# Attention scores in one orientation instead of two, on one Trainium2 core

## The reference

```python
xn = layernorm(x)
q_latent, kv_latent = xn @ wq_down, xn @ wkv_down            # 192 and 64 wide
q = concat(q_latent @ wq_nope, rope(q_latent @ wq_rope))     # 16 heads, 128 + 64
k = concat(kv_latent @ wk_nope, rope(kv_latent @ wk_rope))
v = kv_latent @ wv_up                                        # 16 heads, 192
probs = softmax(where(causal, q @ k.T / sqrt(192), -inf))    # per batch and head
x + (probs @ v) @ wo + expert_mix(xn)     # 32 gated experts, top 8 of them per token
```

## Time and profile before

| Profiled execution | |
|---|---|
| device time | 1277.71 us |
| span of the trace | 1275.9 us |
| mean granted clock of the matrix engine | 0.985 |
| matrix engine busy | 1216.7 us (95%), 5952 products |
| VectorE busy | 898.6 us (70%) |
| ScalarE busy | 589.5 us (46%) |
| GpSimd busy | 682.0 us (53%) |

### The profile page before, as it was taken

One profiled execution on the slowest core, in us unless ns is written; L12 is line 12 of the kernel. 1 busy time (PEld: TensorE's weight loads), 2 busy tenths in 40 slices (PEclk: granted clock), 3 DMA queues, 4 the chain that ended last, 5 costly groups with the idle time before them and its releaser, 6 DMA issues. The chain is left out here.

```text
span 1275.9 us, 20266 instructions
## 1 busy us (share of the span) xinstructions
PE 1216.7 (95%) x5952; PEld 809.1 (63%) x5952; DVE 898.6 (70%) x1410; ACT 589.5 (46%) x1192; POOL 682.0 (53%) x546
## 2 busy tenths in 40 slices
PE   5899899999999999999999999979999999999997
PEld 3555465555565555555655555547888887888886
DVE  6679879879889888888888798664544444544444
ACT  3454536545546445456355365443434343333332
POOL 1176667677677667767776676552233333233332
PEclk9988999999999999999999999998999999999999
DMA  5001001001000000000000001006533334433332
GB/s 202 34 1 33 1 1 33 1 1 32 0 0 17 15 0 15 16 0 2 30 0 0 15 0 58 1 26 180 163 115 107 110 115 114 127 109 115 115 115 90
DMA packets 26442, 67.33 MB, mean 53 GB/s; under 512 B 3044, under 2 KB 9700, under 8 KB 26408
## 3 DMA queue, kind: packets, MB, share of 16 engines
q1 hardware_dynamic: 26264, 66.84, 17.4%
q10 hardware_dynamic: 144, 0.07, 0.0%
HBM read 62.42 MB, written 4.47 MB: 52 GB/s over the span
## 5 line engine op out<-in xcount | busy, mean ns | idle before, releaser
L734 ACT ACTIVATE ring<-ps_s 128x512 f32<-128x512 f32 (+3 forms) x320 | 146.5, 468 | 302.3 <-PE ps_s L601 301.2
L1333 POOL TENSOR_TENSOR hl<-hf,hh 128x512 fp32r<-128x512 f32 x96 | 123.5, 1286 | 288.2 <-ACT hh L1270 288.2
L897 DVE TENSOR_REDUCE nm<-ps_m 128x1 f32<-128x512 f32 (+3 forms) x370 | 197.8, 550 | 47.0 <-PE ps_m L569 42.1
L1060 POOL TENSOR_TENSOR first<-first,ring 128x512 f32<-128x512 f32 (+3 forms) x160 | 159.5, 997 | 83.8 <-ACT ring L734 51.2
L1029 POOL TENSOR_TENSOR xtf<-xtf,sinv 128x512 f32<-128x512 f32 x62 | 85.3, 1375 | 119.3 <-DVE xtf L851 119.3
L1302 DVE TENSOR_TENSOR gs<-gs,routing 128x512 f32<-128x512 f32 x64 | 44.3, 692 | 137.8 <-ACT gs L1266 137.8
L908 DVE TENSOR_TENSOR first<-first,ring 128x512 f32<-128x512 f32 (+3 forms) x160 | 133.1, 832 | 9.7 <-ACT ring L734 4.9
L613 PE MATMUL ps_o<-ring,kvn 128*64 128x512 f32 (+3 forms) x640 | 132.6, 493 | 0.0
L598 PE MATMUL ps_s<-shift,ones 128*128 128x512 bf16 (+3 forms) x384 | 126.7, 330 | 0.2 <-ACT first L734 0.2
L1270 ACT ACTIVATE hh<-hf 128x512 fp32r<-128x512 f32 x96 | 60.7, 633 | 122.0 <-DVE hf L1307 122.0
L1266 ACT ACTIVATE gs<-ps_g 128x512 f32<-128x512 f32 x96 | 57.4, 598 | 121.4 <-PE ps_g L1225 121.4
(11 more groups left out here) (241 smaller groups left out, 3104.3 us busy)
## 6 DMA issues: line engine op xcount, KB each, us to landing
routing<-wT_scratch SPq DMA_DIRECT2D x34, 256.0 KB, 3.7
raw_a<-in_e SPq DMA_DIRECT2D x17, 384.0 KB, 3.0
cosv<-in_e SPq DMA_DIRECT2D x17, 384.0 KB, 3.0
sinv<-wT_scratch SPq DMA_DIRECT2D x17, 384.0 KB, 3.6
raw<-in_e SPq DMA_DIRECT2D x17, 384.0 KB, 3.0
routing<-wT_scratch SPq DMA_DIRECT2D x16, 384.0 KB, 3.3
raw_a<-in_a SPq DMA_DIRECT2D x8, 512.0 KB, 3.4
raw_b<-in_b SPq DMA_DIRECT2D x8, 480.0 KB, 4.0
```

What stands on the lines that cost most here:

```text
L734: nc.scalar.activation(probs(k, e), ps_s[(2 * k + e) % 3][:, off:], ACT.Exp, scale=SCALE).then_inc(exp_done, 1)
L897: nc.vector.tensor_reduce(out=to, in_=bank[:, 0:keys], axis=AXX, op=ALU.max, negate=True).then_inc(piece_max, 1)
L1060: nc.gpsimd.tensor_tensor(first[:, c, 1, off:], first[:, c, 1, off:], probs(k, 1), ALU.add).then_inc(sum_pool, 1)
L1333: nc.gpsimd.tensor_tensor(hl[:, c, :], hf[:, c, :], hh[:, c, :].bitcast(F32), ALU.subtract).then_inc(h_lo, 1)
```

## The change

The scores are computed once, with **queries on partitions**. The unit is now a tile `t` of 128 queries (8 per stage, `TILES`) with all its `(t + 1) * 128` keys as the moving operand. A tile over more than 512 keys (`t >= 4`) goes as two halves of equal width into two neighbouring banks. So the eight banks are now two per head for scores (`ps_s`), two for transposes (`ps_t`), `ps_o` and one `ps_x`.

- VectorE reduces both halves of a head's scores in one instruction to `nm`, the negated maximum (`maximum`).
- ScalarE takes the exponential with `nm` as bias, and the same instruction gives the row sum into `lsum` (`exponent`). The scale is folded into the keys in `prepare`.
- The probabilities are then turned, 128 by 128, by the matrix engine (`turn`, with `ident`), and copied to SBUF by ScalarE (bank `ps_t0`) or VectorE (bank `ps_t1`) (`take_turned`), and only then multiplied with the values (`values`), now 128 queries at a time.
- VectorE inverts the 8 columns of sums (`invert`), ScalarE spreads them (`widen`), the matrix engine turns them (`spread`), ScalarE copies them (`take_reciprocals`), and VectorE multiplies.
- Gone are the 24 pieces and their maxima, `shift` and its product, `add_probs` on VectorE and GpSimd, the product with ones, and the reciprocal over 512 columns.

The first six projections go to six different free banks (`start_banks`). The core of the diff:

```diff
+            def scores(i, b, t, e, half):
...
+                if half == 0:
+                    ge(pe, exp_done, u - 1)
...
+                nc.tensor.matmul(out[:, 0:width], qhi[b][e][:, q], khi[b][e][:, kk], start=not diagonal, stop=False, skip_group_check=True)
+                nc.tensor.matmul(out[:, 0:width], qhi[b][e][:, q], klo[b][e][:, kk], start=False, stop=False, skip_group_check=True)
+                mm = nc.tensor.matmul(out[:, 0:width], qlo[b][e][:, q], khi[b][e][:, kk], start=False, stop=True, skip_group_check=True)
+            def turn(s, t, e, g):
+                x = g if t >= TPC else e
+                before = s * TURNS_PER_S + turns_before(t) + (e if t >= TPC else 0)
+                pe.wait_ge(exp_done, s * U + 2 * t + e + 1)
+                ge(pe, copied[x], before)
+                for at, j in enumerate(groups_of(t)[g]):
+                    mm = nc.tensor.transpose(ps_t[x][:, at * P:(at + 1) * P], prob[t % 2][e][:, j * P:(j + 1) * P], ident[:, :])
+                mm.then_inc(turned[x], 1)
+            def values(s, b, t):
+                for x in range(2):
+                    pe.wait_ge(copied[x], s * TURNS_PER_S + turns_before(t + 1))
...
+                for j in range(t + 1):
+                    for e in range(2):
+                        mm = nc.tensor.matmul(ps_o[64 * e:64 * e + 64, at], kvn[:, b * 8 + j, :], pt[t % 2][:, e, j, :], start=j == 0, stop=j == t)
...
+                        else:
+                            for e in range(2):
+                                scores(i, b, t, e, 0)
+                                scores(i, b, t, e, 1)
+                            turn(sp, tp, 0, 0)
+                            turn(sp, tp, 0, 1)
+                            also(("KR1", "Yp1", "WA")[t - TPC - 1])
+                            turn(sp, tp, 1, 0)
+                            turn(sp, tp, 1, 1)
+                            if t == TILES - 1:
+                                also("Y0")
+                            values(sp, bp, tp)
+                            also(("QL1", "B", "Y1")[t - TPC - 1])
...
+                nc.scalar.activation(prob[t % 2][e][:, 0:len(halves) * width].rearrange("p (h k) -> p h k", k=width),
+                                     ps_s[e][:, 0:len(halves), 0:width], ACT.Exp, bias=nm[:, e:e + 1],
+                                     accum_out=lsum[:, t // TPC, t % TPC, e:e + 1]).then_inc(exp_done, 1)
...
+                        exponent(s, t, 0)
+                        if t > TPC:
+                            take_turned(sp, tp, 0, 0)
...
+                        if has and (t == 0 or t > TPC):
+                            take_turned(sp, tp, 1, 0)
+                        exponent(s, t, 1)
...
+                        if 0 < t < TPC:
+                            maximum(s, t, 0)
+                            take_turned(sp, tp, 1, 0)
```

More of the change, by code:

```diff
@@ L303, in misc_order @@
             got.append((b, name))
+            if last and b and name == "Lp":
+                got += [(b, turn) for turn in TURNS]
     return got
@@ L603, in values @@
-            def values(s, b, k, alone=False):
-                c, j, off, _ = step_of(k)
-                last = k in (TPC - 1, STEPS - 1)
-                if j == 0:
-                    ge(pe, o_copied, s * 2 + c)
-                for e in range(2):
-                    if e or alone:
-                        pe.wait_ge(exp_done, s * U + 2 * k + e + 1)
-                    nc.tensor.matmul(ps_o[64 * e:64 * e + 64, off:], kvn[:, b * 8 + j, :], probs(k, e),
-                                     start=j == 0, stop=last).then_inc(pv_done, 1)
@@ L627, in row_sums, with spread @@
-            def row_sums(i, b, name, s, c):
-                for e in range(2):
-                    pe.wait_ge(*sums(s, c, 7 if c else 3, e))
-                def products(out):
-                    for e in range(2):
-                        mm = nc.tensor.matmul(out[64 * e:64 * e + 64, :], ones[:, 0:64], first[:, c, e, :], start=True, stop=True)
+                        mm = nc.tensor.transpose(out[0:E, j * P:(j + 1) * P], w2[:, g * TPC + j, :], ident[:, :])
                     return mm
                 side(i, b, name, products)
+            def spread(out):
+                for t in range(TPC):
+                    mm = nc.tensor.transpose(out[:, t * P:(t + 1) * P], rec[:, t * P:(t + 1) * P], ident[:, :])
+                return mm
@@ L640, in project_out @@
                 pe.wait_ge(olo_done, s * 2 + c + 1)
[L642 to L647 removed]
+                side(i, b, name, lambda out: out_products(out, m))
             def body(i):
@@ L694, in _ @@
             for name in PROLOGUE:
                 project(0, None, name, 0, 0)
-            for n in range(NP):
-                piece(0, n, 0)
             pairs_loop(pe, body)
-            s = 2 * PAIRS - 1
-            values(s, 1, STEPS - 1, alone=True)
-            n = BEFORE_LAST + len(LAST)
+            s, t = 2 * PAIRS - 1, TILES - 1
             for e in range(2):
-                pe.wait_ge(*sums(s, 1, 7, e))
+                for g in range(2):
+                    turn(s, t, e, g)
+            pe.wait_ge(widened, s * 2 + 2)
```

732 lines of the change are left out of this document (345 added, 387 removed).

## The result

The changed kernel takes 1356.9 us (median of 4 runs, 1353.41 to 1367.88), the kernel before 1276.46 us. The ratio is 1.0643, with a 95% interval of 1.0579 to 1.0707: slower by 6.4%. Beside two of the later kernels it was timed once more: 1357.7 us, ratio 1.0627 (1.0603 to 1.0651). The forecast was 1333 us, its own range 1300 to 1365. The profiled execution took 1353.4 us at a span of 1351.6.

The account below looks back on a forecast made before the run. The matrix engine bounds the kernel, hardly waiting. Profiled 1277.7 us, +64 for 15 longer stages, -5.7 start, -4 first stage, +1.8 last stage gives 1334, median 1333 us; own range 1300 to 1365, overall 1225 to 1410.

Parts of the forecast that it names:

- the 0.5 us allowed for row sums: Each stage: 0.5 us added for the exponential's row sums and for double waits in front of an instruction.
- the third rival: Value products: up to 32 dense 128-column records run slower than 0.053 us each; 1398 us, at the far end 1460; chance 11%.
- first product: Start: first score product waits only for GpSimd's low part, ready at 69.35 us instead of starting at 75.04: -5.7 us.
- first stage: First attention stage: no turns and values of an earlier stage, so -4 us.
- 14 stages: Attention stages at 53.9 us each: 43.0 of matrix-engine work, 10.4 of waits, 0.5 for the rest.
- last stage, to the output product: Last stage without projections: 36.7 us to the last score, then tile 7's chain, together 44.8 against 43.0 before: +1.8 us.
- The second rival: Tiles 0 to 3: waits drop the clock, 6 us of work per stage at 1.2 GHz; +48 us, 1381 us; chance 14%.
- the 4 us that I took off: First stage: 4 us less because it has no turns and values of an earlier stage.
- The faster rival: Tiles 3, 5 and 6: VectorE and ScalarE clear low parts earlier, half the waits remain; 1247 us; chance 24%.

Follow-up runs that it names:

- the last and fastest version: Changed kernel with values one tile later, values between the heads' turns, ScalarE's first copy ahead of the exponential, and reciprocals turned later: 1218.8 us, ratio 0.9536.

## Why the prediction was right, and where the 24 us are

**The mechanism.** It was that of the forecast: less work for the matrix engine, and more waiting than is saved, since each copy stands behind work of the next tile. Moving the values alone, with the same products, took the 85 us away again, so this is shown and not only argued. The waits came where they were placed. Forecast and measured idle time before the instruction, in us:

| tile | forecast | measured | waits for |
|---|---|---|---|
| 0 | 1.0 | 0.19 + 0.88 | reciprocals; VectorE's copy |
| 1, 2 | 1.1, 0.8 | 0.82, 0.58 | VectorE's copy |
| 3 | 1.7 | 1.74 | VectorE's copy behind low parts |
| 4 | 1.0 | 0.83 | reciprocals |
| 5 | 0.7 + 0.9 | 0.40 + 0.82 | ScalarE's copies |
| 6 | 1.4 + 0.8 | 1.34 + 0.74 | ScalarE's, VectorE's copy |
| 7 | 1.4 in every second stage | 0.8 in each | splits of `WA` in one, ScalarE's copy in the other |

The rows' idle time begins when the last product has passed, 0.17 us after the queue was empty (a row of 0.28 us at a distance of 0.11). With this added to some eleven waits a stage, the 8.9 us measured are 10.8 in the forecast's way of counting, which had 10.4 and 0.5 for the rest. Of the 54.05 us of a stage this leaves 43.3 us of work, and the forecast had 43.0. That the stage was hit within 0.2 us is in part luck: most of the 0.5 us allowed for row sums was not there (0.15 us by the run without them), and the waits were as much longer.

**The work.** Seven turns take 0.76 us, 0.109 each (forecast 0.113):

```profile
335.44 0.93 PE L559 MATMUL ps_t<-ident,prob 128*128 128x128 f32 x7
336.20 1.00 PE L64 MATMUL ps_x<-raw_a 128*128 128x64 f32 x8
```

32 value records in a row take 1.90 us (forecast 32 x 0.053 + 0.36 = 2.06):

```profile
400.43 1.97 PE L571 MATMUL ps_o<-pt,kvn 128*64 128x128 f32 x32 [0.88 <-DVE pt L876]
402.33 0.50 PE L520 MATMUL ps_x<-q1hi,rhi 128*128 128x512 f32 x1
```

So the third rival is out, and the row of four records was the better guide: 0.059 us each, with the group's own cost in it. The Trainium skill's figure for a stream, about 81 ns ("TensorE: Matmul & The Clock Gate", Back-to-back issue gap), does not hold for these records, whose weights are 64 columns wide.

**The sum**, along the profiled execution, in us:

| term | forecast | measured |
|---|---|---|
| first product | 69.35 | 69.60 |
| first stage | 49.9 | 51.5 |
| 14 stages | 14 x 53.9 = 754.6 | 766.3 |
| last stage, to the output product | 44.8 | 51.15 |
| from there to the end of the span, against before | 0 | -1.2 |
| median of the runs, against the profiled one | -1.0 | +3.5 |

The marks are these rows:

```profile
69.60 0.27 PE L545 MATMUL ps_s<-ident,mask 128*128 128x128 bf16 x1 [14.22 <-POOL keys L1036]
...
121.08 0.23 PE L545 MATMUL ps_s<-ident,mask 128*128 128x128 bf16 x1
...
887.37 0.23 PE L545 MATMUL ps_s<-ident,mask 128*128 128x128 bf16 x1
...
938.52 0.50 PE L598 MATMUL ps_x<-ohi,bhi 128*128 128x512 f32 x1 [2.23 <-DVE olo L1010]
```

The 14 stages: 14 x 54.05 = 756.7 us would be the undisturbed ones, 2 us off. The other 10 us are six falls of the clock (6 to 7), and the second stage, which with a fall and longer waits in it takes 56.4 us (121.08 to 177.49). The second rival thus came true in a small part. It had 6 us of slow work in every stage; it was 3.4 us in less than every second one. The prediction's reason against it, that single waits stay under 2 us, did not hold: one of 1.74 us was enough. That part is also what makes the runs scatter: 1353.4 us at a clock of 0.981, 1367.9 at 0.970. The median therefore lies above the profiled execution and not below it, another 4.5 us.

The last stage is a mis-sized term of mine. The last score ends at 925.10 (924.71 + 0.39), a good estimate (37.7 us against 36.7). For what follows I counted only tile 7's own chain, 8.1 us. It took 13.4:

```profile
926.72 0.96 PE L559 MATMUL ps_t<-ident,prob 128*128 128x128 f32 x7 [0.85 <-ACT pt L723]
...
928.42 1.75 PE L571 MATMUL ps_o<-pt,kvn 128*64 128x128 f32 x28
930.10 0.50 PE L598 MATMUL ps_x<-ohi,bhi 128*128 128x512 f32 x1
...
932.28 1.16 PE L559 MATMUL ps_t<-ident,prob 128*128 128x128 f32 x8 [0.34 <-ACT pt L723]
...
934.31 1.97 PE L571 MATMUL ps_o<-pt,kvn 128*64 128x128 f32 x32 [0.44 <-DVE pt L876]
```

Behind the last score the matrix engine still owes tile 6's turns and values and two output products, until 930.90. Only then come tile 7's turns, in two rounds through two banks. A unit that lags by one is paid in full at the end.

In the first stage the clock is at half until 75.9 us. And of the 4 us that I took off for the work of an earlier stage, some comes back as waiting: without `Yp1` ahead of it, head 1's first turn in tile 6 waits 2.12 us in place of 1.34.

**The faster rival** (1247 us, waits absorbed) failed since the engines keep their order however idle they are. What the runs added is that it takes only moves within the three lists to make it true: 1243 and 1219 us.

## What to carry to other kernels

When a change lightens the busiest engine but puts two more hand-overs between its products, sum the waits by laying out each queue, not the loads. An idle engine is no cover if what is wanted stands behind the next unit's work. Give each link of such a chain a whole unit of lag first (here values two tiles behind the scores: 85 us of 1357, with no more memory), and then look at what each copy stands behind. And count, behind the last unit, all that the lag has left over.

## What the runs showed of the hardware that was not expected

- **Short waits move the clock.** Waits of 1.34 and 0.74 us with 0.87 us of turns between them are enough to be followed, in some stages, by 3.4 us at 1.2 GHz, and so is a single wait of 1.74 us. Ten unused products in the first wait left no fall in its tile; the kernel became faster by 9 us (0.7%), not all of it in these tiles, and its runs agree within 1.4 us.
- **A loop's branch can stop the matrix engine.** In the profiled execution of the last and fastest version the record of its branch at the end of an attention pair lasts 3.75 us once and 3.37 us another time; in the eleven other traces none is over 0.3 us. The profile puts this idle time down to GpSimd, which had long signalled:

```profile
432.19 0.39 PE L605 MATMUL ps_x<-ohi,blo 128*128 128x512 f32 x1
435.92 0.29 PE L550 MATMUL ps_s<-ident,mask 128*128 128x128 bf16 x1 [3.35 <-POOL qlo L1048]
```

```profile
432.00:435.00 3.00, 0.58 (x3) 0.14 (x1) 0.85 (x2) 2.49 (x4) 2.24 (x2) 0.73 0.03 5
435.00:438.00 3.00, 2.08 (x11) 2.04 (x11) 0.29 (x1) 0.14 (x1) 2.70 (x3) 0.50 0.02 5
```

  Two stages in this execution are 7.6 and 6.3 us longer for it, the break and some 10 and 7 us at half the clock behind it. In the same trace the instruction queue q8 moved 28 packets between 190 and 820 us, in the others 5 to 11. That the branch waited for code is what these two facts suggest; no run tests it.
- **The sum that an exponential puts out is an instruction of its own**, 0.196 us in the mean and 0.191 to 0.213 us over all widths (104 of them in 350 us).
